# A graph network's attention over source nodes: score, maximum and rescale steps fused on VectorE, the stored maximum moved to ScalarE

## What is computed

```python
lin_x = x @ W_lin.T + b_lin
feat = concatenate([x[src], edge_weights, x[dst]], axis=1)        # 64 + 16 + 64
h = relu(feat @ W_att1.T + b_att1)                                # 144 wide
scores = (h @ W_att2.T + b_att2)[:, 0]
m = segment_max(scores, src)
e = exp(scores - m[src])
alpha = e / segment_sum(e, src)[src]
msg = segment_sum(alpha[:, None] * lin_x[dst], src)
...
```

## Time and profile before

| what | us |
|---|---|
| median of 3 runs | 26938.69 (26914.09 to 26950.12) |
| the profiled execution's own time | 26912.31 |
| its span, first to last instruction | 26910.5 |
| attention over targets, from the first to the last of its steps on DVE | 1069 to 8687 |
| attention over sources, the same | 15256 to 21551 |

### The profile page before, as it was taken

How to read it: one execution, slowest core, us unless ns; L and a number is a source line. 1 busy time by engine, 2 the same in 40 slices (tenths; PEclk the granted TensorE clock), 3 DMA queues, 4 the chain that set the end, 5 groups by cost and what they waited for, 6 DMA issues and landing times. The chain is left out here.

```text
span 26910.5 us, 524609 instructions
## 1 busy us (share of the span) xinstructions
PE 20338.6 (76%) x104364; PEld 13361.9 (50%) x104365; DVE 17234.0 (64%) x58008; ACT 6706.1 (25%) x22583; POOL 16510.4 (61%) x17229
## 2 busy tenths in 40 slices
PE   5688888888887699999999688888888853333334
PEld 2344444444444355555555366666666633333332
DVE  8788888888887544444455677787777753333333
ACT  0233333333333122222222222222222211111111
POOL 0377777777776477777775255555555527777772
PEclk9555555555555555555555566666666655555555
DMA  7122222222225233333335466666666812232233
GB/s 286 29 43 43 43 43 43 43 43 43 43 43 43 46 76 76 76 75 76 76 73 61 63 103 100 102 104 102 102 101 102 96 30 60 60 60 60 60 56 21
DMA packets 2876991, 1889.94 MB, mean 70 GB/s; under 512 B 2008316, under 2 KB 2481378, under 8 KB 2869682
## 3 DMA queue, kind: packets, MB, share of 16 engines
q0 software_dynamic: 607024, 854.80, 21.0%
q1 hardware_dynamic: 2269906, 1034.48, 18.1%
HBM read 1573.79 MB, written 342.46 MB: 71 GB/s over the span
## 5 line engine op out<-in xcount | busy, mean ns | idle before, releaser
L1262 POOL DMA_INDIRECT H<-tab,a_rs x3520 | 3371.3, 958 | 3281.4 <-PE a_ps_a L1410 1793.7
L850 POOL DMA_INDIRECT H<-tab,idx x3520 | 3386.5, 962 | 2052.6 <-issue 1062.7
L1609 POOL DMA_INDIRECT H<-tab,m_idx x3520 | 3352.3, 952 | 1670.8 <-issue 1033.0
L1781 POOL DMA_INDIRECT g_G<-tab,g_rs x3520 | 3328.9, 946 | 1622.8 <-issue 1073.7
L1843 PE MATMUL g_ps_a<-g_zr,g_oh 128*128 128x64 f32 x7040 | 1712.6, 425 | 2870.2 <-issue 2040.6
L1533 POOL DMA_INDIRECT rec<-PT,posi x3125 | 3058.9, 979 | 1280.2 <-issue 1028.8
L1843 PEld LDWEIGHTS g_ps_a<-g_zr,g_oh 128*128 128x128 f32 x7040 | 1567.0, 328 | 3016.2 <-issue 2231.8
L928 DVE CUSTOM_DVE_ANT_0 junk<-ps_lb,pen 128x512 bf16<-128x512 f32 x3520 | 2291.8, 689 | 849.3 <-PE ps_lb L1035 803.3
L1709 PEld LDWEIGHTS m_ps_a<-m_Sx,H 128*128 128x128 f32 x7040 | 1567.3, 328 | 1415.6 <-issue 1415.0
L1067 PEld LDWEIGHTS ps_a<-V,H 128*128 128x128 f32 x7040 | 1567.3, 328 | 763.0 <-issue 763.0
L1800 DVE TENSOR_TENSOR g_z<-g_ps_e,g_G 128x256 f32<-128x256 f32 x880 | 373.9, 425 | 2413.7 <-DMA g_G<-tab,g_rs 2413.7
(11 more groups left out here) (330 smaller groups left out, 37922.2 us busy)
## 6 DMA issues: line engine op xcount, KB each, us to landing
a_rs<-rec SPq DMA_DIRECT2D x880, 164.0 KB
g_rs<-rec SPq DMA_DIRECT2D x880, 164.0 KB
rec<-H SPq DMA_DIRECT2D x46, 3116.0 KB
m_row<-key SPq DMA_DIRECT2D x880, 128.0 KB
H<-startp SPq DMA_DIRECT2D x880, 128.0 KB
a_row<-keyc SPq DMA_DIRECT2D x880, 128.0 KB, 4.1
PT<-in_ea SPq DMA_DIRECT2D x625, 160.0 KB
H<-tab,idx POOLq DMA_INDIRECT x3520
```

The lines of the kernel that those rows point to most:

```text
L850: pool.indirect_dma_start(G[:, k, t, :], None, table, bass.IndirectOffsetOnAxis(ap=idx[:, k, t, :], axis=0)).then_inc(s_g[k], 16)
L1262: pool.indirect_dma_start(G[:, k % SLOTS, t, 0:R], None, tab2, bass.IndirectOffsetOnAxis(ap=rs[:, k, t, 1:2], axis=0)).then_inc(s_g[k % SL ...
L1609: pool.indirect_dma_start(G[:, k, t, :], None, tab1, bass.IndirectOffsetOnAxis(ap=idx[:, k, t, :], axis=0)).then_inc(s_g[k], 16)
L1781: pool.indirect_dma_start(G[:, k, t, :], None, tab3, bass.IndirectOffsetOnAxis(ap=rs[:, k, t, 1:2], axis=0)).then_inc(s_g[k], 16)
```

## The change

In attention over sources:

- `scores`: the two additions of 128x288 become one of 128x576. The relu-and-multiply of 128x576 and the separate sum become four instructions of 128x144, each of which also gives the sum of its row (accum_out).
- `maxima`: the maximum of the group starts from the old maximum, which stands ready in a small tile `mo`, so that one instruction gives a_mn. The separate new maximum, the step and the copy into M are gone from DVE.
- `keep`: rescale and addition are one instruction.
- ACT's `rescale` computes exp(mo - mn) directly. It also copies a_mn into M, waits for that copy, and copies the next group's old maximum out of M into `mo`. Both copies need a register load of the group's block number.
- a_ps_a has two buffers, and `node_sums` of g-1 waits for `keep` of g-3 instead of g-2.

In attention over targets: ACT writes the keys and places of a set five groups before its scatter, not three (at k = 0 and k = 2, both one round ahead).

The diff, without the list of semaphores:

```diff
@@ -76,9 +76,9 @@
     return (g - by, (k - by) % SLOTS, r if k >= by else r - 1)
 
 
-def after(g, k, r):
-
-    return (g + 1, (k + 1) % SLOTS, r if k < SLOTS - 1 else r + 1)
+def after(g, k, r, unroll=SLOTS):
+
+    return (g + 1, (k + 1) % unroll, r if k < unroll - 1 else r + 1)
 
 
 def stage(f, lag, n, g, k, r, unroll=SLOTS):
@@ -801,7 +801,7 @@
                     "edge_max", "score_less_max", "exponent", "weight", "values", "group_sums", "acc_rescaled", "group_done", "max_high", "max_low"))
                 s_lb = [seml(f"scores_spread{h}_") for h in range(heads)]
                 if layer == 0:
-                    filler = scatter_fill(ctx, 2, 0, (1, 3), (2, 0), (1, 0), ROUNDS)
+                    filler = scatter_fill(ctx, 2, 0, (1, 3), (0, 2), (1, 1), ROUNDS)
                 else:
                     filler = None
                 s_gm = [seml(f"group_max{h}_") for h in range(heads)]
@@ -1187,9 +1187,8 @@
                 lg = sbl("lg", [P, T])
                 hi = sbl("hi", [P, T], BF16)
                 junk = sbl("junk", [P, GE], BF16)
-                gm = sbl("gm", [P, 1])
                 mn = sbl("mn", [P, 1], BF16)
-                df = sbl("df", [P, 1])
+                mo = sbl("mo", [P, 2])
                 corr = sbl("corr", [P, SLOTS])
                 dd = sbl("dd", [P, T])
                 p = sbl("p", [P, T])
@@ -1198,16 +1197,16 @@
                 ps_z = ps_in(ctx, "a_ps_z", [P, 2, 512])
                 ps_lb = ps_in(ctx, "a_ps_lb", [P, GE])
                 ps_m = ps_in(ctx, "a_ps_m", [P, 512])
-                ps_a = ps_in(ctx, "a_ps_a", [P, 512])
+                ps_a = ps_in(ctx, "a_ps_a", [P, 2, 512])
                 zv = [ps_z[:, b, 0:tpb * width].rearrange("p (t c) -> p t c", t=tpb) for b in range(2)]
                 lbv = ps_lb[:].rearrange("n (p t) -> n t p", t=T)
 
...
@@ -1282,16 +1281,16 @@
                             dve.wait_ge(s_g[k % SLOTS], uses(k, r) * (16 * T))
                             at_least(dve, s_sum, g)
                             settle(dve)
-                            for b in range(2):
-                                ts = slice(b * tpb, (b + 1) * tpb)
-                                ins = dve.tensor_tensor(z[:, ts, :], zv[b], G[:, k % SLOTS, ts, 0:width], ALU.add)
-                            ins.then_inc(s_act, 1)
+                            dve.tensor_tensor(z[:].rearrange("p (b t) c -> p b t c", b=2),
+                                              ps_z[:, :, 0:tpb * width].rearrange("p b (t c) -> p b t c", t=tpb),
+                                              G[:, k % SLOTS, :, 0:width].rearrange("p (b t) c -> p b t c", b=2), ALU.add).then_inc(s_act, 1)
                             dve.wait_ge(s_act, g + 1)
-                            dve.scalar_tensor_tensor(z[:], z[:], 0.0, bcast(att, 1, T), ALU.max, ALU.mult).then_inc(s_mul, 1)
-                            dve.wait_ge(s_mul, g + 1)
                             at_least(dve, s_lg, g)
                             at_least(dve, s_hi, g)
-                            dve.tensor_reduce(ss[:], z[:], AX.X, ALU.add).then_inc(s_sum, 1)
+                            settle(dve)
+                            for t in range(T):
+                                ins = dve.scalar_tensor_tensor(z[:, t, :], z[:, t, :], 0.0, att, ALU.max, ALU.mult, accum_out=ss[:, t:t + 1])
+                            ins.then_inc(s_sum, 1)
 
                         def weighted(g, k, r):
                             dve.wait_ge(s_p, g + 1)
@@ -1304,23 +1303,13 @@
                             return dve.value_load(blk[0:1, 1, bass.ds(g, 1)], min_val=0, max_val=NB)
 
                         def maxima(g, k, r, b):
-                            m_old = M[:, bass.ds(b, 1)]
                             dve.wait_ge(s_lb, g + 1)
                             dve.wait_ge(s_pen, g + 1)
-                            at_least(dve, s_mn, g)
-                            settle(dve)
-                            dve.tensor_tensor_reduce(junk[:], ps_lb[:], pen[:, k % 2], 1.0, -LOW, ALU.add, ALU.max, gm[:]).then_inc(s_gm, 1)
-                            dve.wait_ge(s_gm, g + 1)
+                            dve.wait_ge(s_mo, g + 1)
                             at_least(dve, s_mb, g)
                             at_least(dve, s_me, g)
                             settle(dve)
-                            dve.tensor_tensor(mn[:], m_old, gm[:], ALU.max).then_inc(s_mn, 1)
-                            dve.wait_ge(s_mn, g + 1)
-                            at_least(dve, s_corr, g)
-                            dve.tensor_tensor(df[:], m_old, mn[:], ALU.subtract).then_inc(s_df, 1)
-                            dve.wait_ge(s_df, g + 1)
-                            settle(dve)
-                            dve.tensor_copy(m_old, mn[:]).then_inc(s_mb, 1)
+                            dve.tensor_tensor_reduce(junk[:], ps_lb[:], pen[:, k % 2], 1.0, mo[:, k % 2:k % 2 + 1], ALU.add, ALU.max, mn[:]).then_inc(s_mn, 1)
 
                         def exponents(g, k, r):
                             dve.wait_ge(s_me, g + 1)
@@ -1335,11 +1324,10 @@
                         def keep(g, k, r, b):
                             acc = ACC[:, bass.ds(b, 1), 0:VC].rearrange("p a c -> p (a c)")
                             dve.wait_ge(s_corr, g + 1)
+                            dve.wait_ge(s_acc, g + 1)
                             at_least(dve, s_done, g)
-                            dve.tensor_scalar(acc, acc, corr[:, k % SLOTS:k % SLOTS + 1], None, ALU.mult).then_inc(s_sc, 1)
-                            dve.wait_ge(s_sc, g + 1)
-                            dve.wait_ge(s_acc, g + 1)
-                            dve.tensor_tensor(acc, acc, ps_a[:, 0:VC], ALU.add).then_inc(s_done, 1)
+                            settle(dve)
+                            dve.scalar_tensor_tensor(acc, acc, corr[:, k % SLOTS:k % SLOTS + 1], ps_a[:, k % 2, 0:VC], ALU.mult, ALU.add).then_inc(s_done, 1)
 
                         blocks = [None] * U
 
@@ -1390,7 +1378,7 @@
 
                         def spread(g, k, r):
                             pe.wait_ge(s_hi, g + 1)
-                            at_least(pe, s_gm, g)
+                            at_least(pe, s_mn, g)
                             for t in range(T):
                                 mm = pe.matmul(lbv[:, t, :], hi[:, t:t + 1].broadcast_to([P, P]), identb[:], start=True, stop=True)
                             mm.then_inc(s_lb, 1)
@@ -1405,9 +1393,9 @@
 
                         def node_sums(g, k, r):
                             pe.wait_ge(s_oh, g + 1)
-                            at_least(pe, s_done, g)
+                            at_least(pe, s_done, g - 1)
                             for t in range(T):
-                                mm = pe.matmul(ps_a[:, 0:VC], oh[:, k % SLOTS, t, :], G[:, k % SLOTS, t, v0:R + 1],
+                                mm = pe.matmul(ps_a[:, k % 2, 0:VC], oh[:, k % SLOTS, t, :], G[:, k % SLOTS, t, v0:R + 1],
                                                start=(t == 0), stop=(t == T - 1))
                             mm.then_inc(s_acc, 1)
 
@@ -1446,7 +1434,7 @@
 
                         def penalty(g, k, r):
                             act.wait_ge(s_ohN, g + 1)
-                            at_least(act, s_gm, g - 1)
+                            at_least(act, s_mn, g - 1)
                             act.activation(pen[:, k % 2], ohN[:, k % SLOTS], ACT.Copy, bias=-LOW, scale=LOW).then_inc(s_pen, 1)
 
                         def high_part(g, k, r):
@@ -1457,9 +1445,21 @@
                             act.activation(lg[:], ss[:], ACT.Identity, bias=rows[:, ROWS["b_att2"]]).then_inc(s_lg, 1)
 
                         def rescale(g, k, r):
-                            act.wait_ge(s_df, g + 1)
-                            at_least(act, s_sc, g - SLOTS + 1)
-                            act.activation(corr[:, k % SLOTS:k % SLOTS + 1], df[:], ACT.Exp).then_inc(s_corr, 1)
+                            act.wait_ge(s_mn, g + 1)
+                            at_least(act, s_done, g - SLOTS + 1)
+                            settle(act)
+                            act.activation(corr[:, k % SLOTS:k % SLOTS + 1], mn[:], ACT.Exp, bias=mo[:, k % 2:k % 2 + 1], scale=-1.0).then_inc(s_corr, 1)
+                            act.copy(M[:, bass.ds(block_of(g), 1)], mn[:]).then_inc(s_mb, 1)
+                            if not is_group(g, NG - 1):
+                                act.wait_ge(s_mb, g + 1)
+                                old_maximum(*after(g, k, r, U))
+
+                        def block_of(g):
+                            return act.value_load(blk[0:1, 1, bass.ds(g, 1)], min_val=0, max_val=NB)
+
+                        def old_maximum(g, k, r):
+                            at_least(act, s_corr, g - 1)
+                            act.copy(mo[:, k % 2:k % 2 + 1], M[:, bass.ds(block_of(g), 1)]).then_inc(s_mo, 1)
 
                         def weights(g, k, r):
```

(14 more changed lines are left out.)

## The result

The changed kernel takes 27,141.86 us (median of 5, 27,051.94 to 27,174.67) where the kernel before takes 26,938.69: a ratio of 1.0068, 95% interval 1.0048 to 1.0088. It is 0.7% slower. The forecast was 26,100, and its range ended at 26,740. The profiled execution took 27,068.89 us, its span 27,067.1.

The account below looks back on a forecast made before the run. Attention over sources was taken as bound by a loop between PE and DVE, neither full; 880 groups at 6.19 us give 5450 against 6295, 845 saved, so 26,100 us in all, range 25,550 to 26,740.

Parts of the forecast that it names:

- the sum itself: Attention over sources: 880 groups at 6.19 us make 5450 us against 6295, 845 us saved.
- rival 4: Attention over sources: ScalarE's weight p comes late and bounds the loop, 7.5 us a group, 27,250 us; chance 0.05.
- with the same 44% of long groups: Attention over sources: 44% of groups take 6.95 us and 56% take 5.6, mean 6.2 us.
- rival 2: Attention over sources: the clock falls, all groups take PE's 6.95 us, stage 6116 us, total 26,760; chance 0.18.
- rival 1: Attention over sources: the clock rises, most groups take 5.6 us, stage 4930 us, total 25,570; chance 0.2.
- The maximum to the kept sum: DVE in attention over sources: from 2.10 us to 1.0 us a group, 1.1 saved.
- Scores: DVE in attention over sources: pass and sum of 1.54 us become four instructions of 1.2 us together, 0.3 saved.
- rival 3: Attention over sources: the four short score instructions take 1.8 us, 6.5 us a group, total 26,395; chance 0.13.
- `node_sums`: PE in attention over sources: with two buffers its 0.83 us of idle time a group go.
- ScalarE: Attention over sources: from a_mn to weight p about 2.0 us, hidden; uncovered it would cost up to 1 us a group.
- Attention over targets: Earlier writing of the scatter's keys costs 0, with 20 us either way; some 8 us to spare.
- rival 5: Attention over targets: ACT stalls for scatters, 1 us in each of 440 writes, half hidden, 220 us lost; chance 0.02.

Follow-up runs that it names:

- 16 idle instructions: The changed kernel with 16 already-met wait instructions on VectorE, run once ahead of the loop over sources: 26,375 us, 0.9784 of before.
- the old scores: The changed kernel with scores as one pass plus one reduction again, and 68 already-met waits ahead of its loop over sources: 26,613 us, 0.9878 of before.
- 80 idle instructions: The changed kernel with 80 already-met wait instructions on VectorE, run once ahead of the loop over sources: 26,674 us, 0.9902 of before.
- the old targets: The changed kernel with the targets' scatter keys written as before: 35,754 us (1.005) on the slower chip; with 16 idle instructions, 26,346 us (0.9770) on the other.

## Why the prediction was wrong

**The step that failed** is the sum itself, "880 x 6.19 = 5450 us against 6295". It adds up what stands within a group and has no term for the loop that eight groups form, nor for where in DVE's program that loop lies. The part on the change named it nowhere: it costed each step that was moved and never the instructions' own transfer. The stage over sources lost 725 us to it (6370 against 5645; 762 in the medians on one chip), more than the whole difference in sign. The rivals had no such case either; rival 4, the one on the slower side, put the loss on ScalarE's weight p. It is refuted by the view of p's line, L1467: p was waited for once in 880 groups.

```profile
who waited for it (us, times):
  DVE H L1299: 0.3, 1
```

The rule that bears on it stands in the Trainium skill, Runtime: NRT & Kernel Launch, Instruction fetch mechanics: a branch taken back to a block that is no longer on the engine waits for its transfer. The runs agree as to that: DVE's idle time at a return is 4.3 to 8.2 us in the medians of the runs with fetches, and 0.5 with 16 idle instructions. The page says two blocks of 16 KiB; here packets are 8 KB and loops of 327 and 342 instructions stay when they touch three of them and don't at four. The measurement decides.

**Without the stall, the mechanism was right and one size off.** The stage then takes 5645 us against the 5450 of the sum; before took 6288. By the maximum's starts in the run with 16 idle instructions:

```profile
18002.81 0.75 DVE L1314 CUSTOM_DVE_ANT_0 a_junk<-a_ps_lb,a_pen,a_mo 128x512 bf16<-128x512 f32 x1 [1.62 <-PE a_ps_lb L1385]
18007.88 0.74 DVE L1314 CUSTOM_DVE_ANT_0 a_junk<-a_ps_lb,a_pen,a_mo 128x512 bf16<-128x512 f32 x1
...
18043.35 0.75 DVE L1314 CUSTOM_DVE_ANT_0 a_junk<-a_ps_lb,a_pen,a_mo 128x512 bf16<-128x512 f32 x1 [1.27 <-PE a_ps_lb L1385]
18050.12 0.75 DVE L1314 CUSTOM_DVE_ANT_0 a_junk<-a_ps_lb,a_pen,a_mo 128x512 bf16<-128x512 f32 x1 [1.63 <-PE a_ps_lb L1385]
```

The rows show both kinds, 5.1 us from the first to the second and 6.8 between the last two. Over the stage, a group wholly at the lower clock takes 6.8 us in the median (the sum had 6.95), one wholly at the higher 5.3 (the sum had 5.6). What was mis-sized is "with the same 44% of long groups": a mean of 6.42 from 5.3 and 6.8 stands for about three quarters, and by the clock 518 of 879 groups ran wholly at 1.2 GHz where before 102 did. The granted clock of the stage fell from 0.65 to 0.62. The gain of each group was partly paid back in clock, on the way to rival 2 (6116 us, never a high group); rival 1, most groups high, did not come. What decides the share stays open: the clock was 0.54 with the old scores, whose groups are longer, and 0.66 with the stalls of 80 idle instructions.

The sum also had no term for the gathers. DVE waited for them ahead of the addition for 168.9 us in 155 groups (view above, 16 idle instructions). Before:

```profile
  DMA H<-tab,a_rs: 35.5, 29
```

The 133 us more are at most two thirds of the 195 us by which 5645 misses 5450. POOL's four gathers are near a limit of their own in the fast groups, 1.25 us apart without a longer pause and so 5.0 us a group:

```profile
18011.59 0.95 POOL L1261 DMA_INDIRECT H<-tab,a_rs  x1 [0.30 <-issue]
18012.85 0.94 POOL L1261 DMA_INDIRECT H<-tab,a_rs  x1 [0.30 <-issue]
```

No run here made the gathers faster, so this share is argued.

**The steps one by one.** *The maximum to the kept sum*: 18000.75 to 18001.70, 0.95 us, of the 1.0 forecast. *Scores*: four from 18011.61 to about 18012.6, 1.0 us, of the 1.2 forecast and the 1.54 before; rival 3 does not happen: it needed 1.8 us, and an instruction of 144 columns is followed by the next after 0.23 us. *`node_sums`*: its idle time fell from 743 us to 0.1, as forecast, but not by the second buffer (above). *ScalarE*: from a_mn at 18001.5 to p at 18003.47, 2.0 us as forecast, and hidden:

```profile
18001.63 0.29 ACT L1451 ACTIVATE a_corr<-a_mn,a_mo 128x1 f32<-128x1 bf16 x1 [0.74 <-DVE a_mn L1312]
18002.25 0.19 ACT L1452 CAST a_M<-a_mn 128x1 bf16 x1 [0.33 <-issue]
18003.17 0.19 ACT L1462 COPY a_mo<-a_M 128x1 f32 x1 [0.73 <-ACT a_M L1452]
18003.27 0.20 ACT L1467 ACTIVATE a_p<-a_dd 128x4 f32<-128x4 f32 x1
```

**Attention over targets** was taken at 0 with 20 us either way, and grew by 76 us (first to last addition 1069.6 to 8678.9 before, 1072.9 to 8757.9 after). With 16 idle instructions and the old places of the keys it is 7609 us again, with the new ones 7677, on one chip, so the keys' place is the cause. A wait of ScalarE for a scatter (rival 5) does not show; two small DVE instructions are longer. Before, after, and with the old targets again:

```profile
L954 DVE TENSOR_SCALAR dd<-dd 128x16 f32<-128x16 f32 x880 | 163.4, 186 | 30.1
L937 DVE CAST mnp<-mn 128x4 bf16<-128x4 f32 x880 | 150.2, 171 | 30.0
```

```profile
L954 DVE TENSOR_SCALAR dd<-dd 128x16 f32<-128x16 f32 x880 | 220.6, 251 | 30.1
L937 DVE CAST mnp<-mn 128x4 bf16<-128x4 f32 x880 | 215.9, 245 | 30.0
```

```profile
L954 DVE TENSOR_SCALAR dd<-dd 128x16 f32<-128x16 f32 x880 | 162.5, 185 | 30.1
L937 DVE CAST mnp<-mn 128x4 bf16<-128x4 f32 x880 | 149.3, 170 | 30.0
```

139 ns more in each of 880 groups are 123 us; a third step, L869, gets back 76 (290.0 to 214.1 us). The net 47 us are more than half of the growth; the rest I did not trace. In the changed kernel's trace from 2000 to 8000 us the time of L937 goes by when it begins: 170 ns in the first 0.6 us of a POOL gather or scatter instruction, 297 on average when 0.6 to 0.8 us into one, 233 when behind its end (but 172 behind the end in the run with 16 idle instructions, so that part of the pattern doesn't hold). The change shifted POOL's instructions against DVE's. The Trainium skill, SBUF — State Buffer, SBUF: two separate sides, has these two engines share one pair of ports, which a DVE instruction in a two-port mode, or with two inputs in SBUF, holds for its whole length, as does a GpSimd one. The two rows have a single source; whether they ran in such a mode no run here shows, so that the port is the cause is argued and was not tried. In the medians of whole kernels the old place is worth 28 us (26,346 against 26,375), less than the runs of either spread.

## What to carry to other kernels

When a loop's body is changed, count the instructions of each engine from one return to the next, and look at the profile's row of instruction packets: a number that grows with the rounds of a loop says that the loop is fetched again at each return, and moving it by a few instructions can be worth more than the change. Judge a fused kernel only after that: here it stood 0.7% behind and, moved by two instructions, 2% ahead. And the share of groups at the high clock is not to be carried over from one form to the next: the clock of this stage was 0.65 before, 0.62 with the whole change and 16 idle instructions, 0.54 with all but the new scores.

## What was not expected of the hardware

A fetch at the return costs DVE 8.2 us (median) where the loop's first instruction is the last of its block, and 5.4 to 5.9 where the edge is further on; on the slower chip 7.2 and 4.3. In the changed kernel's trace DVE's first register instruction runs 5.6 us after the branch and the next 2.4 us later.

On one chip the kernels took 26 to 33% longer. There DVE and ScalarE wait 5 to 6 us for TensorE's results again and again in the attention over targets, and the profile names what ends these waits only "remote", as here in the changed kernel with the old targets:

```profile
4984.70 0.17 DVE L949 TENSOR_TENSOR dd<-lg,ps_m 128x16 f32<-128x16 f32 x1 [5.00 <-remote]
...
4991.77 0.26 ACT L1096 COPY eaT<-ps_ea 64x128 f32<-64x128 f32 x1 [6.34 <-remote]
```

On that chip the places of the scatter's keys five groups ahead were worth 1679 us (35,014 against 33,335). That POOL had more to do ahead while the others stood is a guess; no run tries it, and what delays the results stays open. The changed kernel itself did not run there; by its old-targets form less 1679 us it would be about 4% ahead of before, an estimate. The best version measured on the other chip is the one with the loop moved, with the old or the new places of the keys.
